# A decoder layer on one core: cross-attention scores from 32-row quarters of TensorE into four banks, a third of the keys at a time

## The reference, cut to what matters

```
x = x + attention(layernorm(x))                        # self-attention, 16 heads of 16
x = x + cross_attention(layernorm(x), ctx)             # below
x = x + nvfp4_ffn(layernorm(x))                        # fake-quantized gate, up, down

# cross-attention, x [16, 112, 256], ctx [16, 375, 256], H = 16 heads of 16
Q = split_heads(query @ Wq + bq);  K = split_heads(key @ Wk + bk);  V = split_heads(value @ Wv + bv)
energy = einsum('bhqd,bhkd->bhqk', Q, K) / sqrt(16)
energy = where(mask == 0, -1e10, energy)               # mask [16, 1, 112, 375]
attention = softmax(energy, axis=1)                    # over the 16 heads, not over the keys
x = einsum('bhqk,bhkd->bhqd', attention, V) ... @ Wo + bo
```

## Time and profile before

| | us |
|---|---|
| median of 3 runs | 657.27 (655.97 to 659.51) |
| profiled execution, its own time | 656.48 |
| span of the profiled execution | 654.6 |
| PE busy | 553.0 (84%) |
| DVE busy | 534.7 (82%) |
| POOL busy | 364.1 (56%) |
| ACT busy | 309.5 (47%) |

### The profile page before, as it was taken

How to read it: one execution, slowest core, us unless ns; L and a number is a source line. 1 busy time by engine, 2 the same in 40 slices (tenths; PEclk the granted TensorE clock), 3 DMA queues, 4 the chain that set the end, 5 groups by cost and what they waited for, 6 DMA issues and landing times. The chain is left out here.

```text
span 654.6 us, 14337 instructions
## 1 busy us (share of the span) xinstructions
PE 553.0 (84%) x5904; PEld 380.5 (58%) x5904; DVE 534.7 (82%) x781; ACT 309.5 (47%) x505; POOL 364.1 (56%) x272
## 2 busy tenths in 40 slices
PE   4799999995799999999999999999999773666543
PEld 3677777763566666666566566766666431333222
DVE  4687888887387877898988989888998969999983
ACT  3566666662254444455444453445353352545431
POOL 6402332223266566667775886588668545596552
PEclk9999999999799999999999999999999886877765
DMA  8910000000100110111011101110110000000000
GB/s 190 301 50 2 2 3 3 2 2 1 46 1 1 52 52 9 46 52 54 8 46 52 51 4 53 53 47 10 49 52 10 1 14 1 2 16 33 10 22 34
DMA packets 18611, 23.44 MB, mean 36 GB/s; under 512 B 2997, under 2 KB 16290, under 8 KB 18546
## 3 DMA queue, kind: packets, MB, share of 16 engines
q1 hardware_dynamic: 16626, 21.73, 11.3%
q10 hardware_dynamic: 1920, 0.79, 0.6%
HBM read 18.85 MB, written 1.84 MB: 32 GB/s over the span
## 5 line engine op out<-in xcount | busy, mean ns | idle before, releaser
L1126 POOL TENSOR_TENSOR work<-work,rden 125x1792 f32<-125x1792 f32 x48 | 178.7, 3723 | 99.8 <-DVE rden L785 99.2
L976 ACT ACTIVATE work<-scores 125x896 f32<-125x896 f32 x96 | 95.1, 990 | 112.9 <-PE scores L1260 112.4
L774 DVE TENSOR_REDUCE negmax<-scores 125x56 bf16<-125x896 f32 x96 | 104.3, 1086 | 51.3 <-PE scores L1250 50.9
L783 DVE TENSOR_REDUCE den<-work 125x56 f32<-125x896 f32 x96 | 103.2, 1075 | 0.0
L1250 PE MATMUL scores<-qz,kT 64*125 64x224 f32 x768 | 89.0, 350 | 0.0
L1250 PEld LDWEIGHTS scores<-qz,kT 64*125 64x125 f32 x768 | 72.1, 184 | 0.8
L1275 PE MATMUL head_out<-work,v 125*32 125x112 f32 x1536 | 57.8, 271 | 4.1 <-POOL work L1126 3.8
L1260 PE MATMUL scores<-negmax,identb 125*125 125x448 bf16 x192 | 54.0, 362 | 6.7 <-DVE negmax L774 6.6
L1275 PEld LDWEIGHTS head_out<-work,v 125*32 125x32 f32 x1536 | 37.8, 109 | 28.6 <-issue 20.6
L785 DVE RECIPROCAL rden<-den 125x56 f32<-125x56 f32 x96 | 48.3, 503 | 3.3
L324 DVE TENSOR_REDUCE a_mpad<-a_s_ps 112x8 bf16<-112x896 f32 x32 | 33.5, 1092 | 20.7 <-PE a_s_ps L498 20.7
(11 more groups left out here) (186 smaller groups left out, 1088.7 us busy)
## 6 DMA issues: line engine op xcount, KB each, us to landing
ctx_sb<-in_ctx SPq DMA_DIRECT2D x16, 375.0 KB
mask_sb<-in_mask_Bx1xSxS_if SPq DMA_DIRECT2D x32, 164.1 KB
xsx<-in_x SPq DMA_DIRECT2D x4, 448.0 KB, 9.5
out_x<-ores SPq DMA_DIRECT2D x7, 256.0 KB, 2.2
a_raw_w<-in_L_ffn_gate_w SPq DMA_DIRECT2D x1, 1024.0 KB, 6.2
a_raw_w<-in_L_ffn_up_w SPq DMA_DIRECT2D x1, 1024.0 KB, 8.7
a_raw_w<-in_L_ffn_down_w SPq DMA_DIRECT2D x1, 1024.0 KB, 12.3
xt<-xsx SPq DMA_DIRECT2D x4, 112.0 KB, 2.2
```

The lines of the kernel that those rows point to most:

```text
L774: dve.tensor_reduce(negmax[0:KP, u, :], scores[u][0:KP, :, 0:HM * HALF].rearrange("p a (h t) -> p t a h", h=HM), AX.XY, ALU.max, negate=Tr ...
L783: link(dve.tensor_reduce(den[0:KP, kc, half], ex2[0:KP, kc, :, half, :].rearrange("p g t s -> p t g s"), AX.XY, ALU.add))
L976: act.activation(ex2[0:KP, kc, :, u * HALF:(u + 1) * HALF, :].rearrange("p (a g) t s -> p a g s t", a=2), scores[u][0:KP, :, 0:HM * HALF]. ...
L1126: pool.tensor_tensor(ex2[0:KP, kc], ex2[0:KP, kc], over, ALU.mult).then_inc(s["prob"], 1)
```

## The change

- One unit is a whole third: 16 heads, 112 tokens, in four banks. `scores` is one tile of four banks instead of two of two.
- `score(q, kc)`: the penalties are eight matmuls of 224 columns; the scores are eight fp32 matmuls on 32 rows each, four row quarters side by side, one bank each. `own_queries` makes `qz` with two heads per 32 rows in one instruction of 448 values instead of two.
- One maximum per third (`key_max`), four less_max matmuls, two exponentials (`half_exp`: two banks each), two head sums that wait for both exponentials, one reciprocal (`inverse`).
- TensorE refills banks 0 and 1 after the first exponential, banks 2 and 3 after the second.
- All six weight transposes go to turn -1, into the score banks, copied by ScalarE (even) and VectorE (odd); `score` of batch 0 waits for all of them.
- `residual` moves one turn later, and SP's packing DMAs with it; `x_shift` and `x_normal` go from a pair's first turn to its second. The order on all four engines is new.
- In `head_outputs` the four column quarters take turns.

The diff of the functions, cut to its core:

```diff
-                    for n in range(2):
-                        pe.matmul(scores[u][0:KP, n, 0:HM * HALF], pen[64 * n:64 * n + HALF, r, u, kc, :],
-                                  identb[64 * n:64 * n + HALF, 64 * n:64 * n + HALF].unsqueeze(1).to_broadcast([HALF, HM, HALF]),
-                                  start=True, stop=False, skip_group_check=True)
+                def score(q, kc):
+
+
+
+                    b, r, _ = q
+                    for i in range(2):
+                        wait(pe, s["exp"], 6 * b + 2 * kc - 1 + i)
+                        for u in range(2):
+                            for n in range(2):
+                                bank = scores[0:KP, 2 * i + n, 0:4 * TOK].rearrange("p (a t) -> p a t", t=TOK)
+                                pe.matmul(bank[:, :, u * HALF:(u + 1) * HALF], pen[64 * n:64 * n + HALF, r, u, kc, :],
+                                          identb[64 * n:64 * n + HALF, 64 * n:64 * n + HALF].unsqueeze(1).to_broadcast([HALF, 4, HALF]),
+                                          start=(u == 0), stop=False, skip_group_check=True)
                     for m in range(NE):
-                        for n in range(2):
-                            rows = slice(64 * n, 64 * n + 64)
-                            last = pe.matmul(scores[u][0:KP, n, m * GROUP * HALF:(m + 1) * GROUP * HALF],
+                        for j in range(4):
+                            rows = slice(32 * j, 32 * j + 32)
+                            last = pe.matmul(scores[0:KP, j % 2 * 2 + j // 2, m * 2 * TOK:(m + 1) * 2 * TOK],
                                              kT[rows, r, m, kc * KP:(kc + 1) * KP],
-                                             qz4[rows, r, m, :, u * HALF:(u + 1) * HALF],
+                                             qz[rows, r, m].rearrange("p s t -> p (s t)"),
                                              start=False, stop=False, skip_group_check=True)
                     last.then_inc(s["s_ps"], 1)
 
-                def less_max(q, kc, u):
-                    b, r, _ = q
-                    wait(pe, s["max"], 6 * b + 2 * kc + u + 1)
-                    for m in range(NE):
-                        last = pe.matmul(scores[u][0:KP, m, 0:HM * HALF], identb[0:KP, 0:KP],
-                                         negmax[0:KP, u, :].unsqueeze(1).to_broadcast([KP, HM, HALF]),
+                def less_max(q, kc):
+                    b, r, _ = q
+                    wait(pe, s["max"], 3 * b + kc + 1)
+                    for j in range(4):
+                        last = pe.matmul(scores[0:KP, j, 0:4 * TOK], identb[0:KP, 0:KP],
+                                         negmax[0:KP, :].unsqueeze(1).to_broadcast([KP, 4, TOK]),
                                          start=False, stop=True, skip_group_check=True)
-                    last.then_inc(s["sm_ps"], 1)
+                        if j % 2:
+                            last.then_inc(s["sm_ps"], 1)
...
+                    for n in range(2):
+                        for j in range(4):
+                            h = chunk * HM + 2 * j + n
+                            last = pe.matmul(pair_output(h), pair_values(KP, r, kc, h), ex2[0:KP, kc, j % 2 * 4 + j // 2 * 2 + chunk, :, n],
+                                             start=(kc == 0 and chunk == 0 and n == 0),
+                                             stop=(kc == NKC - 1 and n == 1), skip_group_check=True)
...
+                def weight_piece(i):
+                    dve.wait_ge(s["wT_ps"], i + 1)
+                    dve.tensor_copy(weight_half(i), wT_ps(i)).then_inc(s["w_dve"], 1)
+
+                def key_max(q, kc):
+                    b, r, _ = q
+                    wait(dve, s["s_ps"], 3 * b + kc + 1)
+                    dve.tensor_reduce(negmax[0:KP, :],
+                                      scores[0:KP, :, 0:4 * TOK].rearrange("p j (h t) -> p t j h", h=4),
                                       AX.XY, ALU.max, negate=True).then_inc(s["max"], 1)
...
-                    wait(dve, s["exp"], 6 * b + 2 * kc + u + 1)
+                    wait(dve, s["exp"], 6 * b + 2 * kc + 2)
...
+                def inverse(q, kc):
+                    b, r, _ = q
+                    dve.reciprocal(rden[0:KP, kc, :], den[0:KP, kc, :]).then_inc(s["rden"], 1)
...
-                def unit_exp(q, kc, u):
-                    b, r, _ = q
-                    wait(act, s["sm_ps"], 6 * b + 2 * kc + u + 1)
+                def half_exp(q, kc, i):
+                    b, r, _ = q
+                    wait(act, s["sm_ps"], 6 * b + 2 * kc + i + 1)
                     wait(act, s["pv"], 3 * b + kc - 2)
-                    act.activation(ex2[0:KP, kc, :, u * HALF:(u + 1) * HALF, :].rearrange("p (a g) t s -> p a g s t", a=2),
-                                   scores[u][0:KP, :, 0:HM * HALF].rearrange("p a (g s t) -> p a g s t", s=2, t=HALF),
+                    act.activation(ex2[0:KP, kc, 4 * i:4 * i + 4].rearrange("p (j m) t s -> p j m s t", m=NE),
+                                   scores[0:KP, 2 * i:2 * i + 2, 0:4 * TOK].rearrange("p j (m s t) -> p j m s t", m=NE, s=2),
                                    ACT.Exp).then_inc(s["exp"], 1)
 
...
-                    wait(pool, s["s_ps"], 6 * b - 6)
-                    wait(pool, s["small_read"], query_reads(b))
-                    for m in range(NE):
-                        pool.tensor_tensor(qz4[:, r, m], qT[:, r, m].unsqueeze(1).to_broadcast([P, GROUP, TOK]),
-                                           own4[:].unsqueeze(2).to_broadcast([P, GROUP, TOK]),
-                                           ALU.mult).then_inc(s["qz"], 1)
+                    wait(pool, s["s_ps"], 3 * b - 3)
+                    wait(pool, s["small_read"], 2 * b + 2)
+                    pool.tensor_tensor(qz[:, r], qT[:, r].unsqueeze(2).to_broadcast([P, NE, 2, TOK]),
+                                       own2[:].unsqueeze(1).unsqueeze(3).to_broadcast([P, NE, 2, TOK]),
+                                       ALU.mult).then_inc(s["qz"], 1)
...
-                for n in range(B + 1):
+                for n in range(B + 2):
                     if n + 1 >= 2 and n + 1 < B:
                         wait(sp, s["ctxT_ps"], n)
                         load_context(sp, n + 1, (n + 1) % 2)
                         wait(sp, s["pen"], n)
                         load_mask(sp, n + 1, (n + 1) % 2)
-                    if n >= 1:
-                        sp.wait_ge(s["x2"], n)
+                    if n >= 2:
+                        sp.wait_ge(s["x2"], n - 1)
                         for b, row, tile, off, rows in pieces():
-                            if b == n - 1:
+                            if b == n - 2:
                                 sp.dma_start(xt[off:off + rows, tile, :], xs[row:row + rows, b, :]
                                              ).then_inc(x_in[tile // 2], 16)
```

248 lines of the change are left out of this document (115 added, 133 removed).

## The result

| | before | after |
|---|---|---|
| median | 656.88 us of 4 runs (655.97 to 659.51) | 682.05 us of 4 runs (677.64 to 685.95) |
| span of the profiled execution | 654.6 us | 684.2 us |

A forecast was written before the change was run, and what follows sets the result against it. TensorE's queue was taken as the bound in cross-attention. From 656.5 us: -3.7 for the stage (48.6 of stalls included), +5 start, +5 tail, +4 clock gave 666.8, or 667.6 against the median; range 636 to 688.

The forecast's parts named there:

- The held instructions: VectorE, turns 4 to 15: two-input instructions behind a reciprocal wait for GpSimd's normalisation; 48.6 us of stalls together.
- The plain turn: Cross-attention turns without FFN pairs: a serial chain of 6.19 us per third, 18.6 per batch against 21.4, VectorE hidden.
- Clock: TensorE's granted clock falls after stalls from turn 5 on; +4 us uncovered (bounds 0 and 20), 1.8 of it turn 11.
- the rival of 25 us for the clock: Clock falls at each of some 14 stalls, nothing covering it: 25 us in place of 4, total 688; chance 0.13.
- Start: Before the first scores: score(0, 0) waits for all weight copies and transposes; +5 us (bounds 3 and 8).
- Tail: From the last maximum to the first hidden: x_rounded and x_shift held by normalisations; +5 us (bounds 0 and 7).
- Get in ahead of GpSimd: Rival: VectorE's two-input instructions start before GpSimd and take free durations; stalls 14.3 us, total about 625; chance 0.22.
- The chain is longer in every third: Rival: tiling switch and later wake-ups lengthen each third; +11 to 15 us, total about 680; chance 0.12.
- the tiling switch at 0.33: TensorE, scores after penalties of another row tile: 0.33 us per third as upper bound, where the forecast took 0.1.
- the later wake-ups: Second reason for a longer chain in every third, beside the tiling switch; together +11 to 15 us, chance 0.12.
- The quarters apart: Rival: the four 32-row score quarters do not run together on TensorE; +43 us, total 710; chance 0.03.
- The signs put down ahead: Right: plain turns 18 to 19 us, held instructions over 3; wrong: turns above 20, first maximum later than 182.

The follow-up runs named there:

- Experiment 3: Kernel after with x_shift, x_shifted, x_variance and x_rounded all moved ahead of the reciprocals, in the last turn too; 643.78 us, ratio 0.9787 to the kernel before.
- experiment 2: Kernel after with one edit, x_shift moved ahead of inverse(old, 2); 674.24 us, ratio 1.0260 to the kernel before.
- experiment 5: Experiment 3 with the six weight transposes and copies back in turns 0 to 5, one to a turn; 636.22 us, ratio 0.9660.
- experiment 4: Kernel after with scores from 64-row halves, two side by side, and queries masked four heads wide again; 713.58 us, ratio 1.0859.
- Experiment 6: Experiment 5 with the dequantiser's reciprocal (x_inverse) moved behind the next turn's first maximum; 636.36 us, ratio 0.9667.
- experiment 8 with the penalties: Experiment 5 with VectorE's penalty selection put ahead of variance, rounding and reciprocal, penalty matmuls still issued; 634.37 us, ratio 0.9663.
- Experiments 1: The kernel after run once more, unchanged, for its spread; 684.08 us, ratio 1.0399 to the kernel before.

## Why the prediction came out as it did

The direction, the mechanism and the tail were right; the size was short by 14 us in the median (682.05 against 667.6), 19 in the profiled execution (685.95 against 666.8). The 19 are 17.1 in the plain length of the turns, 4.6 ahead of cross-attention and 0.8 in the tail, less 3.0 by which held instructions and clock stayed below their 52.6, and 0.35 at the start.

- **The held instructions: right.** Forecast 48.6 us of stalls, and 4 more for the clock. Measured over plain turns of 19.57 us, the table above gives 2.5 (turn 4) + 15.3 (five turns) + 20.9 (three) + 3.2 (10) + 3.9 (11) + 3.8 (15) = 49.6, the clock in it. Experiment 3 divides it: 12.8 stay there, the work that these turns have in any order, and 36.8 go. By kind: turns 6, 8 and 13 took 6.95 more (forecast 7.9), the five 3.06 (3.0), turn 10 3.2 (4.2), turn 4 2.5 and turn 11 3.9 (0.75 each), 1.4 of the last by the clock. So the total is near by errors that cancel in part, and one is a miss of kind: x_variance was not expected to be held, since it reads one tensor. It took 3336 ns on average in the groups above, and where it stands ahead of x_rounded it took the hold that was forecast for that one, which was held in turn 10 alone. Here the Trainium skill is fuller than the prediction's reading of the earlier trace rows: SBUF — State Buffer, "SBUF: two separate sides", says that whichever of a VectorE instruction in a two-port mode or with two SBUF inputs, and a GpSimd instruction, starts first keeps the shared port pair for its whole length (with two SBUF inputs, if the GpSimd instruction reads SBUF). The trace agrees, with a two-element `tensor_scalar` of 3.30 us that ended 0.03 after the normalisation; which mode it was in no run shows. Experiments 2 and 3 show the cause: the same instructions elsewhere, 40 us less.
- **The plain turn: the step that failed.** "So a third is 6.19 us, a batch 18.6": measured 6.41, 6.49 and 6.68, 19.57. The links were the right ones, in the right order; their sizes were short. From the scores' start to the next maximum it was 1.11 to 1.18, not 0.97, and this is the largest miss. The fillers were taken alike, but less_max, all head outputs and the projection are 2.89 (240.81 to 243.70), not 2.74. Penalties and switch came to 0.53 (0.50 forecast). And the sum itself was short: 0.84 + 1.9 + 0.2 is 2.94, which is 0.34 above 2.6 and not 0.25, so the prediction's own links give 6.28. Of the 0.34 us that a third was longer than 6.19, 0.09 is this slip and 0.25 the links. Over 15 turns (0.4 more in turn 0) and two thirds, with the first maximum 2.88 us behind the first penalty at a lowered clock, that is 311.7 us in place of 294.6: +17. The text allowed 0.2 us per third, 10 us in all; the miss was 0.34.
- **Clock: right in kind, smaller.** It fell to 0.50 behind the 4.00 us wait, and the three lines behind it cost 2.24 us more. But the next maximum was held in any case: x_varp ended at 334.28, rounding and a head sum followed without a gap, and the maximum began at 336.23, behind them and not behind TensorE, whose scores had begun at 334.13 and would have let it begin about 1 us earlier. Uncovered the clock cost 1.4 us in turn 11 (forecast 1.8) and little elsewhere: the first intervals of turns 5 and 9, at 0.50, are as long as that of turn 7, at full clock. So it was 1.4 of the 4, and the rival of 25 us for the clock did not happen.
- **Start: right, and one part unseen.** +4.65 for the weights (forecast 5); experiment 5 gives it back. The other +4.6 lies ahead of cross-attention, in code that is the same but for a few start instructions. It was not forecast, and the code alone does not bring it (experiment 2 has the same and came at 167.33); the last section takes it up.
- **Tail: right**, +5.8 against +5, with two held instructions, of which the first was x_variance and not x_rounded.
- **Rivals.** "Get in ahead of GpSimd", 625: it did not happen in the kernel after. Experiment 3 is that case made by hand: 643.8, 19 above its figure, of which the plain turn is 17; its 14.3 us of stalls were 12.8. "The chain is longer in every third", 680, was the nearest rival. Of its two reasons the tiling switch at 0.33 was wrong, since experiment 4 leaves no more than 0.10 for it; the later wake-ups were right in part, in the 1.11 to 1.18 above. The quarters apart, 710: excluded by 0.97 against 1.62.
- **The signs put down ahead.** Plain turns at 19.57 lie between those for right (18 to 19) and for wrong (above 20). x_shift and x_shifted were over 3 us, but x_rounded only in turn 10. The first maximum came at 186.30, past the 182 that was to mean wrong; 4.6 of that is the start ahead of cross-attention.

## What to carry to other kernels

Where VectorE releases GpSimd, put those of VectorE's instructions that were held here (two SBUF inputs, or a `tensor_scalar`) ahead of the release, not behind it: four such moves, with no arithmetic changed, were worth 40 us of 684. When a change replaces an overlapped pair by one serial chain, write down each link and multiply the doubt of one pass through the chain by the number of passes; here 0.34 us was 16. And measure a term by taking it out only after looking at what the shorter chain lets collide.

## What the runs showed of the hardware that was not expected

- A VectorE `tensor_scalar` with one SBUF input is held by a running GpSimd instruction too: about 3.3 us instead of 0.17 for two elements, and 4.41 us instead of 0.58 for the selection of 750 int32 values. GpSimd instructions that follow each other without a gap hold it together: the selection of experiment 4 began in one and ended behind the next. A head sum (`tensor_reduce`, SBUF to SBUF) is not. Experiment 6, order in time, GpSimd and VectorE:

```profile
306.20 3.59 POOL L1130 TENSOR_TENSOR work<-work,rden 125x1792 f32<-125x1792 f32 x1 [4.33 <-DVE rden L785]
...
306.76 1.09 DVE L780 TENSOR_REDUCE den<-work 125x56 f32<-125x896 f32 x1
```

- The first 170 us differ between executions of one code. Of the kernels with the same self-attention, the first cross-attention transpose came at 166.9 to 167.9 us in five profiles and at 169.7 to 171.0 in the other eight. The granted clock from 26 to 34 us goes with it: 0.88 to 1.00 in the five, 0.57 to 0.79 in the eight. That the one causes the other was not tested. The two below are experiment 8 with the penalties and experiment 5, table of stretches; the clock is 0.88 in one and 0.57 in the other over the same 8 us.

```profile
26.00:34.00 8.00, 7.72 (x126) 5.69 (x126) 4.96 (x6) 4.66 (x11) 3.65 (x5) 0.88 0.76 206
```

```profile
26.00:34.00 8.00, 7.81 (x60) 6.36 (x63) 4.25 (x12) 3.64 (x8) 3.01 (x4) 0.57 0.83 227
```

In the kernel after this stretch stands at 0.57 too, in the profile of before at 1.00. What makes an execution take the one or the other was not found. Experiments 1 and 2 have the same code up to there, and the four times of experiment 5 fall in two pairs 5 us apart. Whether the change makes the later start more frequent stays open: the times of the kernel before spread over 2.4 to 7.4 us in their groups as well.
